# One GNN layer with a routed expert layer: the rows of x loaded in their own layout, rows scaled on ScalarE, transposes two tiles ahead, later shared pieces, and the self-loop on VectorE in three of four quarters

## What is computed

```python
deg = max((adj != 0).sum(-1), 1)
x = x + relu((A_norm @ ln(x) + ln(x)) @ W + b)      # A_norm = (adj + I) / deg of the row
x = x + moe(ln(x)) + gelu(ln(x) @ sw1.T) @ sw2.T    # top 1 of 8 experts: silu(w1) * w3, then w2
```

## Time and profile before

| | us |
|---|---|
| median of 3 runs (lowest, highest) | 485.64 (483.78, 487.36) |
| the profiled execution: its own time | 486.0 |
| its span | 484.4 |
| quarter 0, from the first z matmul to the self-loop | 10.35 to 53.70 |
| quarter 1, adjacency tiles | 54.70 to 87.50 |
| quarter 2, adjacency tiles | 114.8 to 139.9 |
| quarter 3, adjacency tiles | 167.7 to 192.9 |
| PE, DVE, ACT, POOL busy | 445.1, 270.8, 203.3, 336.5 |

### The profile page before, as it was taken

The page is one execution under the profiler, slowest core; times in us unless marked ns, Lnnn a source line. Parts: engine busy times, 40 slices in busy tenths (PEclk is TensorE's granted clock), DMA queues, the critical chain, the costliest instruction groups (busy, mean ns, idle before and its releaser), DMA issues.

```text
span 484.4 us, 8954 instructions
## 1 busy us (share of the span) xinstructions
PE 445.1 (92%) x2620; PEld 380.8 (79%) x2621; DVE 270.8 (56%) x549; ACT 203.3 (42%) x449; POOL 336.5 (69%) x309
## 2 busy tenths in 40 slices
PE   5899967999989999979988999999999999999992
PEld 5788845898869878868966888888888888888872
DVE  4998687654974498767773334233433333343330
ACT  3656458464545554574542233222323322232330
POOL 2888947276985799757796467976788579884112
PEclk9999999999999999999998999999999999999998
DMA  7565442201360055568676599997999563644000
GB/s 243 192 210 172 130 129 89 100 1 47 128 216 2 1 167 182 160 217 319 179 225 187 194 393 343 326 339 248 317 326 335 166 244 87 81 61 64 0 1 0
DMA packets 41004, 82.61 MB, mean 171 GB/s; under 512 B 5008, under 2 KB 16656, under 8 KB 38928
## 3 DMA queue, kind: packets, MB, share of 16 engines
q1 hardware_dynamic: 28416, 47.60, 30.1%
q0 software_dynamic: 7536, 29.39, 19.4%
q10 hardware_dynamic: 5024, 5.27, 3.7%
HBM read 74.74 MB, written 8.41 MB: 172 GB/s over the span
## 4 chain that ended last, share of the span: by engine, by line
PE 45%; POOL 19%; issue 9%; DMA 5%; DVE 3%; ACT 3%; SPq 2%; POOLq 1%; ACTq 0%
PE bank L1356 19%; POOL a_lo L447 10%; PE bank L1383 7%; POOL ering L493 5%; PE bank L1275 4%; PE bank L1297 4%; PE bank L1384 4%; DMA ering<-in_experts 3%; PE bank L1369 3%; POOL sorted_x L522 2%; PE bank L1299 2%; DMA eraw<-in_experts 2%; POOL gel_lo L463 2%; SPq L378 1%; ACT a_hi L605 1%
## 5 line engine op out<-in xcount | busy, mean ns | idle before, releaser
L1356 PE MATMUL bank<-ering,xsT_hi 128*128 x368 | 121.6, 402 | 1.9 <-POOL ering L493 1.8
L447 POOL TENSOR_TENSOR a_lo<-araw,a_hi 128x512 fp32r<-128x512 f32 x64 | 97.0, 1533 | 27.7 <-ACT a_hi L605 27.6
L1181 PE MATMUL bank<-zz,a_hi 128*128 128x512 f32 (+1 forms) x256 | 93.0, 402 | 9.8 <-POOL a_lo L447 9.6
L1100 DVE SCALAR_TENSOR_TENSOR hid<-bank,xs,sil 128x512 f32<-128x512 f32 x46 | 34.5, 751 | 92.5 <-ACT sil L740 90.5
L1356 PEld LDWEIGHTS bank<-ering,xsT_hi 128*128 128x128 f32 x368 | 69.9, 190 | 17.5 <-issue 2.7
L493 POOL TENSOR_TENSOR ering<-eraw,ering 128x512 fp32r<-128x512 f32 x40 | 51.9, 1317 | 29.7 <-DMA ering<-in_experts 20.1
L1356 PE MATMUL bank<-ering,xsT_lo 128*128 x184 | 72.4, 393 | 0.0
L1183 PE MATMUL bank<-zz,a_lo 128*128 128x256 f32 (+1 forms) x256 | 71.7, 280 | 0.0
L740 ACT ACTIVATE sil<-bank 128x512 f32<-128x512 f32 x46 | 27.5, 598 | 101.4 <-PE bank L1356 99.3
L1383 PE MATMUL bank<-ering,hidT_hi 128*128 x184 | 67.4, 406 | 1.2 <-DVE hidT_lo L1108 1.2
L1181 PEld LDWEIGHTS bank<-zz,a_hi 128*128 128x128 f32 x256 | 48.0, 188 | 24.2 <-issue 11.7
(11 more groups left out here) (156 smaller groups left out, 826.7 us busy)
## 6 DMA issues: line engine op xcount, KB each, us to landing
araw<-in_adj_t SPq DMA_DIRECT2D x32, 512.0 KB, 3.9
eraw<-in_experts SPq DMA_DIRECT2D x48, 256.0 KB, 5.0
ering<-in_experts POOLq DMA_DIRECT2D x8, 1536.0 KB, 9.0
eraw_more<-in_experts SPq DMA_DIRECT2D x48, 256.0 KB, 5.9
ering<-in_experts POOLq DMA_DIRECT2D x8, 1024.0 KB, 6.7
ering<-in_experts POOLq DMA_DIRECT2D x8, 512.0 KB, 4.8
xs<-sorted_x ACTq DMA_DIRECT2D x20, 129.0 KB, 4.7
resid<-in_x SPq DMA_DIRECT2D x4, 512.0 KB, 9.2
```

What stands on the lines that cost most here:

```text
L447: pool.tensor_tensor(a_lo[:, u % AR, :], araw[:, u // CJ, u % CJ, :], a_hi[:, u % AR, :].bitcast(F32), ALU.subtract).then_inc(adj_lo_ok, 1)
L1181: pe.matmul(acc(q, it)[:, :], a_hi[:, s, it * P:(it + 1) * P], zt, start=first, stop=False)
L1356: ins = pe.matmul(bank[2 * w + h][:, :], a[:, k, :], ering[:, bass.ds(slot, 1), part, at:at + BANK].rearrange("p a n -> p (a n)"), start=n ...
```

## The change

- **x's layout.** The host hands x as (128, 16, 256), so that a partition's rows of several tiles lie together; SP loads tile 0 alone, then tiles 1 to 3, and puts adjacency chunk 0 ahead of the second group.
- **Start.** Tile 0 is normalized alone, the split of W comes ahead of the identity's copy on ACT, and PE makes 10 instead of 20 transposes before it.
- **Rows on ScalarE.** For groups 1 to 3 DVE makes only the scale and the shift (`scales`), and ACT makes the rows as scale * x + shift (`scaled_rows`), three tiles ahead.
- **Transposes two ahead.** PE transposes tile t + 2 after `z_tile(t)`.
- **Bias and self-loop.** POOL no longer adds the bias. In quarters 0 to 2 PE does no `agg_end`, and DVE makes z * (1 + 1/deg) + bias in `first_products`; in quarter 3 the self-loop stays on PE and DVE adds the bias ahead of it (`add_bias`).
- **Shared pieces.** They begin two adjacency tiles later, with four banks for the first four pieces, so that pieces 0 to 3 wait for no earlier piece.
- **Places in the shared part.** Gate and rank steps of two stretches stand one block later, and the shared part waits for `rank_read` in one place only.

```diff
@@ -322,7 +325,7 @@
-            at = bank[2 + i % 2][:, :]
+            at = bank[(2, 3, 0, 1, 2, 3, 2, 3)[i]][:, :]
@@ -338,10 +341,8 @@
         def _(sp):
-            def rows_of_x(g):
-                sp.dma_start(resid[:, g * QT:(g + 1) * QT, :],
-                             x_in[g * QT * P:(g + 1) * QT * P, :].rearrange("(t p) d -> p t d", p=P)
-                             ).then_inc(x_loaded[g], 16)
+            def rows_of_x(first, last, loaded):
+                sp.dma_start(resid[:, first:last, :], x_in[:, first:last, :]).then_inc(loaded, 16)
@@ -353,11 +354,12 @@
-            rows_of_x(0)
+            rows_of_x(0, 1, x_first)
+            rows_of_x(1, QT, x_loaded[0])
...
+                chunk(0, c, c if c >= RAW else None)
...
-                    rows_of_x(c + 1)
-                chunk(0, c, c if c >= RAW else None)
+                    rows_of_x((c + 1) * QT, (c + 2) * QT, x_loaded[c + 1])
@@ -449,11 +451,8 @@
-                pool.wait_ge(bias_loaded, 16)
...
-                    pool.wait_ge(z_copied, t + 1)
-                    pool.tensor_tensor(norm[:, t, :], norm[:, t, :], bias[:], ALU.add).then_inc(bias_added, 1)
@@ -581,10 +580,17 @@
-            def stds(k):
-                act.wait_ge(var_ready, QT * (k + 1))
-                act.activation(std[:], mv[:, :, 1], ACT.Sqrt, bias=eps[:, 0:1]).then_inc(std_ready, 1)
+            def stds(k, first=0, last=QT):
+                act.wait_ge(var_ready, QT * k + last)
+                act.activation(std[:, first:last], mv[:, first:last, 1], ACT.Sqrt, bias=eps[:, 0:1]
+                               ).then_inc(std_ready, 1)
+            def scaled_rows(t):
+                act.wait_ge(scale_ready, t // QT)
+                act.activation(norm[:, t, :], resid[:, t, :], ACT.Identity, bias=shift[:, t % QT:t % QT + 1],
+                               scale=rstd[:, t % QT:t % QT + 1]).then_inc(ln_ready, 1)
@@ -606,21 +612,25 @@
             load_table(ACT.Sqrt)
-            stds(0)
-            act.wait_ge(consts, 1)
-            act.activation(ident_r[:], ident[:], ACT.Copy).then_inc(split_hi, 1)
+            stds(0, 0, 1)
             act.wait_ge(w_loaded, 16)
...
             xn_high(0)
+            stds(0, 1, QT)
+            act.wait_ge(consts, 1)
+            act.activation(ident_r[:], ident[:], ACT.Copy).then_inc(split_hi, 1)
+            xn_high(1)
...
             for t in range(NT):
-                if t % QT == 2 and t // QT + 1 < NQ:
+                if QT <= t + 3 < NT:
+                    scaled_rows(t + 3)
+                z_high(t)
+                if t + 2 < NT:
+                    xn_high(t + 2)
+                adj_high(t % (RAW * CJ), t // (RAW * CJ) + 1, t - AR + 1 if t >= AR else None)
+                if t % QT == 0 and t // QT + 1 < NQ:
                     stds(t // QT + 1)
-                if t + 1 < NT:
-                    xn_high(t + 1)
-                adj_high(t % (RAW * CJ), t // (RAW * CJ) + 1, t - AR + 1 if t >= AR else None)
-                z_high(t)
@@ -635,7 +645,10 @@
-                act.wait_ge(agg_sum, q + 1)
+                if q < NQ - 1:
+                    act.wait_ge(agg_tile, (q + 1) * NT)
+                else:
+                    act.wait_ge(agg_sum, 1)
@@ -682,8 +695,8 @@
-                if i >= 2:
-                    act.wait_ge(sw_lo_ok, i - 1)
+                if i >= 4:
+                    act.wait_ge(sw_lo_ok, i - (3 if i < 6 else 1))
@@ -693,13 +706,12 @@
                     split_gate()
-                for j in range(AR, TURN):
+                for j in range(AR, NT - 1):
                     adj_highs(q, j, j + 1)
-                    if q == 1:
-                        shared_piece_high(j - AR)
+                    if q == 1 and AR + 2 <= j < AR + 10:
+                        shared_piece_high(j - AR - 2)
                     if j == AR + 3:
                         stds(NQ + q - 1)
-                adj_highs(q, TURN, TURN + AR - 1)
                 xfT_highs(q - 1)
@@ -804,13 +816,21 @@
-                if first == 0:
-                    dve.wait_ge(std_ready, k + 1)
-                    chained(dve.reciprocal(rstd[:], std[:]))
-                    settle()
+                dve.wait_ge(std_ready, k + 2 if k > 0 else 1 if first == 0 else 2)
+                chained(dve.reciprocal(rstd[:, first:last], std[:, first:last]))
+                settle()
...
+            def scales(g):
+                dve.wait_ge(std_ready, g + 2)
+                dve.wait_ge(ln_ready, g * QT)
+                chained(dve.reciprocal(rstd[:], std[:]))
+                settle()
+                dve.scalar_tensor_tensor(shift[:], mv[:, :, 0], -1.0, rstd[:], ALU.mult, ALU.mult
+                                         ).then_inc(scale_ready, 1)
@@ -825,6 +845,13 @@
+            def add_bias(q):
+                dve.wait_ge(bias_loaded, 16)
+                dve.wait_ge(z_copied, (q + 1) * QT)
+                for t in group(q):
+                    chained(dve.tensor_tensor(norm[:, t, :], norm[:, t, :], bias[:], ALU.add))
@@ -836,27 +863,34 @@
-            dve.wait_ge(x_loaded[0], 16)
-            variances(group(0))
-            normalize(0, group(0))
+            dve.wait_ge(x_first, 16)
+            statistics(group(0), 0, 1)
+            aggregates(0, 1)
+            normalize(0, group(0), 0, 1)
...
-            dve.wait_ge(split_hi, 2)
+            dve.wait_ge(split_hi, 1)
...
+            dve.wait_ge(x_loaded[0], 16)
+            statistics(group(0), 1, QT)
+            aggregates(1, QT)
+            normalize(0, group(0), 1, QT)
+            xn_low(1)
...
-                if t + 1 < NT:
-                    xn_low(t + 1)
...
-                if g < NQ and i == 0:
-                    dve.wait_ge(x_loaded[g], 16)
-                    dve.wait_ge(ln_ready, g * QT)
-                if g < NQ and i < 2:
-                    statistics(group(g), 2 * i, 2 * i + 2)
-                elif g < NQ:
-                    normalize(g, group(g), 2 * (i - 2), 2 * (i - 1))
...
-                if g < NQ and i == 1:
+                if t + 2 < NT:
+                    xn_low(t + 2)
+                if i == 0 and g < NQ:
+                    if g == 1:
+                        dve.wait_ge(x_loaded[g], 16)
+                        dve.wait_ge(ln_ready, QT)
+                    statistics(group(g), 0 if g == 1 else 2, QT)
...
+                    scales(g)
+                elif i == QT - 1 and g + 1 < NQ:
+                    dve.wait_ge(x_loaded[g + 1], 16)
+                    statistics(group(g + 1), 0, 2)
@@ -888,7 +922,15 @@
-                dve.wait_ge(bias_added, (q + 1) * QT)
+                if q < NQ - 1:
+                    dve.wait_ge(bias_loaded, 16)
+                    dve.wait_ge(z_copied, (q + 1) * QT)
+                    chained(dve.tensor_scalar(self_part[:], dinv2[:], 1.0, None, ALU.add))
+                    settle()
+                    for it, t in enumerate(group(q)):
+                        chained(dve.scalar_tensor_tensor(norm[:, t, :], norm[:, t, :], self_part[:, it:it + 1],
+                                                         bias[:], ALU.mult, ALU.add))
+                settle()
@@ -1002,6 +1044,8 @@
+                if q == NQ - 1:
+                    add_bias(q)
@@ -1201,22 +1245,22 @@
-            keep_clock_up(20)
+            keep_clock_up(10)
...
-                if t + 1 < NT:
-                    xn_transpose(t + 1)
...
+                if t == 0:
+                    xn_transpose(1)
+                if t + 2 < NT:
+                    xn_transpose(t + 2)
...
-                agg_part(0, t, t % AR, t)
+                agg_part(0, t, t % AR, t, last=t == NT - 1)
...
-            pe.wait_ge(z_copied, NT)
-            agg_end(0)
@@ -1226,12 +1270,15 @@
-                    agg_part(q, j, j % AR, q * NT + j)
-                agg_end(q)
+                    agg_part(q, j, j % AR, q * NT + j, last=j == NT - 1 and q < NQ - 1)
+                if q == NQ - 1:
+                    agg_end(q)
...
-                if 0 < q < NQ - 1:
+                if q == 0:
+                    pe.wait_ge(sw_lo_ok, 4)
+                elif q < NQ - 1:
@@ -1283,7 +1330,8 @@
                     pe.wait_ge(agg_free, QT * min(hq // 2 + 2, NQ))
-                    pe.wait_ge(rank_read, min(hq // 2 + 1, NQ - 1))
+                    if hq == 2 * NQ - 3:
+                        pe.wait_ge(rank_read, NQ - 1)
                     if hq == 2 * NQ - 1:
@@ -1333,7 +1381,7 @@
-                    shared((q - 1) * 2 * NI, 2 * NI, {6: lambda: gate_back(q - 1), EARLY_RANKS_AT: lambda: ranks(q - 1)})
+                    shared((q - 1) * 2 * NI, 2 * NI, {7: lambda: gate_back(q - 1), EARLY_RANKS_AT: lambda: ranks(q - 1)})
@@ -1429,7 +1477,7 @@
-        "x": np.asarray(x),
+        "x": np.asarray(x).reshape(-1, P, x.shape[1]).transpose(1, 0, 2),
```

19 lines of the change are left out of this document (11 added, 8 removed).

## The result

The changed kernel takes 490.68 us (median; 489.75 to 491.89) against 486.04 in the same comparison: ratio 1.0101, 95% interval 1.0073 to 1.013. It is slower by 1%, where 479.5 was forecast, and the time lies outside the range. The profiled execution is the slowest of its four (491.89, span 490.2).

A forecast was written before the change was run, and what follows sets the result against it. It took a chain of waits headed by the experts' matmuls as the bound, with only the stretch up to 200 us open to change. 486.0 - 3.4 - 3.0 + 0.3 = 479.9, median 479.5 us; range 476.3 to 484.0.

The forecast's parts named there:

- Term 1, Start: Start of the front: first z near 7.2 us, tile 4's transpose at about 14.9 instead of 17.76.
- the rival by which the start gives nothing: Tile 0 lands no sooner than four tiles did; front gains only 0.8, time 482.1 us; chance 0.10.
- Term 1, Pace: Quarter 0: DVE's group falls from 10.65 to 7.9 us, under PE's 9.66; ScalarE has room for the rows.
- If those waits persist, ScalarE's wait for the scale would stand ahead of z's copies: Sign for the front: explains any PE waits over 0.5 us remaining at the transposes of tiles 8 and 12.
- Term 1, "GpSimd loses the bias ...: nothing": Front: taking the bias from GpSimd gains nothing, since nobody waited for it before the quarter's end.
- Term 2: Quarter 0's end to the shared part, through quarter 1: 32.9 us instead of 35.9, 3.0 less.
- the locks bite fully: Quarter 1: multiply-adds take 5.1 us beside GpSimd, gain shrinks to 0.5, time 482.0 us; chance 0.15.
- DVE fills up in quarter 1: VectorE's additions exceed its idle time; quarter 1 loses 6.7 us, quarter 3 loses 2, median 490.9; chance 0.05.
- Term 3: Quarters 2 and 3: quarter 2 gains nothing, VectorE's bias additions in quarter 3 cost 0.3 us.

The follow-up runs named there:

- e6: Changed kernel with a_hi first in each front tile on ScalarE and the next group's statistics one tile earlier: 487.2 us, ratio 1.0038.
- e3: Changed kernel with ScalarE making a_hi first instead of last in each tile of the front: 488.3 us, ratio 1.0056.
- e2: Kernel before plus only the VectorE self-loop in quarters 0 to 2 and VectorE's bias everywhere, GpSimd's bias additions gone: 491.8 us, ratio 1.0123.
- e5: e1 with a_hi first in each front tile and the next group's statistics one tile earlier: 483.6 us, ratio 0.9942.
- e8: e6 and e7 together, with quarter 3's bias through PSUM as well: 483.0 us, ratio 0.9931.
- e1: Changed kernel with the self-loop back on TensorE in all quarters and the bias back on GpSimd: 487.0 us, ratio 1.0023.
- e7: Changed kernel with the self-loop's products rewritten so that each of the eight has an operand in PSUM: 485.3 us, ratio 0.9992.
- e9: Kernel before plus only the later shared pieces, with own banks for the first four: 482.4 us, ratio 0.9939.
- e4: Changed kernel with the bias of tiles 12 to 15 added by GpSimd in the front instead of VectorE in quarter 3: 491.2 us, ratio 1.0099.
- e12: e11 with the twelve normalized rows of tiles 4 to 15 made by VectorE instead of ScalarE: 483.8 us, ratio 0.9967.
- e10: Changed kernel with 24 small matmuls adding zeros ahead of tile 7 of quarter 1, to keep PE at work: 490.9 us, ratio 1.0127.
- e11: Changed kernel with e6's front, VectorE self-loop only for quarter 1 in e7's form, bias shared between GpSimd and VectorE: 480.4 us, ratio 0.9891.

## Why the forecast was wrong

**Term 1, Start: right, 0.5 late.** T4 at 15.40 for 14.9, and the first z at 7.50 for 7.2; the rival by which the start gives nothing is out. The sum written down gives at most 14.0 + 0.63 = 14.6; the other 0.3 of the 14.9 had no source.

**Term 1, Pace: failed, 3.9 us.** From T4 to the end of quarter 0 are 39.14 us for 35.2. "ScalarE takes on 12 rows of at most 0.63, 7.6 us, on 25.7 busy of 43.35: room enough." The price of a row was right (0.60 to 0.65), ScalarE's busy time stayed under the sum (31.2 for 33.3), and there was room, as e6 shows with the same load. I had counted ScalarE by its sum and not by its queue. A root that waits for DVE's mv, then a row that waits for the scale, stood ahead of z's copies and of a_hi, so the wait of 1.0 that I charged to DVE's group was ScalarE's, and was passed to GpSimd and PE. e3 takes 2.8 of it back, e3's order with earlier statistics 4.15 (34.99 against 39.14). "If those waits persist, ScalarE's wait for the scale would stand ahead of z's copies" was half of it; I had not looked at where a_hi stands.

**Term 1, "GpSimd loses the bias ...: nothing": failed, and it hid part of the miss.** In the front of the kernel before, taking these additions out gave 1.1 (e2, 34.64 for 35.71). In the changed front they cost 1.8 to 1.9 (e5 against e8, e1 against e7), the last four of them 0.7, since the quarter ends in GpSimd's queue. The changed kernel's 39.14 has this gain in it. So it is partly luck that e6's 34.99 comes so near the 35.2 that I worked out: a gain of 1 to 2 us that I had put at nothing is in it, and what takes as much back is not shown.

**Term 2: failed, 5.3 us, by the size of one term and by one that I left out.** New rows were forecast 8.9 after the degrees, with 0.2 for the factor and 2.5 for the multiply-adds; they came after 13.3, with 1.25 and 5.76. The rest of the working came out. From the new rows to tile 13 are 18.2 us in the changed kernel, in e7 and in e8 (13.25 to 31.41, 9.16 to 27.33, 10.22 to 28.40), whatever PE's clock does between. e7, whose new rows come 9.2 after the degrees, took 32.84, where the forecast said 32.9. Behind tile 13 are 5.51 us, or 6.77 where the clock falls behind the wait of 2.27, as in the changed kernel: the other 1.3, which the term did not have. I took 2.5 by the normalizing row of this quarter, beside which GpSimd worked only part of the time, but the multiply-adds stand where GpSimd makes eight a_lo without a break. The bound at 5.1 was the row to take, since GpSimd was always at work beside it, and even that was low. With the pieces at their old place 2.5 would have been near (2.66 in e2).

The rival *the locks bite fully* had the mechanism and nearly the price (5.1). Its quarter 1 would be 35.4; the 2.8 to the measured 38.18 are the multiply-adds' other 0.7, the factor's 1.05 and the clock's 1.3, less 0.2. It let each later microsecond of the new rows count, and e1 and e9 bear that out: the pieces only just meet the new rows at their old time (0.51 and 0.52 of waiting). Its 482.0 still missed, mostly because it kept the front's gain. The Trainium skill (SBUF — State Buffer, Who interferes with whom) says that only the ports which VectorE and GpSimd share make them exclude each other. e7 agrees (0.42 a product with an operand in PSUM, where a multiply-add from SBUF took 1.44), and e2 shows that such a wait can strike a count or an instruction of four elements a row as well.

*DVE fills up in quarter 1* gave the right time (490.9) by luck: it had quarter 1 lose 6.7 and the front gain 3.4, where quarter 1 lost 2.3 and the front 1.1.

**Term 3: off by 0.5.** Quarter 2 gains 0.8 and gives it back, PE's first wait for gel_lo in quarter 3's stretch going from 0.76 to 1.78; that was forecast. The bias additions were 5.8, and cost 0.6 (e4) and not 0.3; the counts behind them, which then ran alone, gave part of it back (2.57 a pair, against 4.55 and 3.43 in e4).

The terms of the miss: start 0.5, pace 3.9, term 2 5.3, term 3 0.5, and 1.6 of the rest, which I take for this execution's spread: 11.8 of the 11.9 between 490.2 and the 478.3 that the forecast gives for the span.

**Not settled.** e1 to e12 don't say what makes the clock fall at one wait of 2.27 and not at another, nor why PE is slow up to 19.7 us in some executions.

## What to carry to other kernels

Before work is put on an engine with room, write down its queue for one tile and ask of each instruction that waits what stands behind it and who needs that; the busy share can't say. Put where GpSimd works without a break, a VectorE instruction that reads two SBUF tensors cost here about one GpSimd instruction (1.44 to 1.5), and even a factor of four elements a row took 1.25: give it an operand in PSUM where it can have one, or put it elsewhere. A price read from a row holds only for the GpSimd work that stood beside that row. When a gain and a loss are in one change, take them apart: the pieces alone, and the rows with another order, were each worth taking.

## What the runs showed of the hardware

- **The same wait, two clocks.** PE waits 2.26 to 2.28 us ahead of tile 13 in the changed kernel and in all the experiments but e2. From there to the degrees are 5.51 us in e3 and e7, 6.73 to 6.79 in the changed kernel, e4, e6, e8, e10, e11 and e12, and with `agg_end(1)` 6.41 and 6.43 in e1 and e5 but 7.76 in e9, whose granted clock of 80 to 85 us was 0.66. The Trainium skill (TensorE: Matmul & The Clock Gate, What's actually happening) has idle time bring the clock down. Here it does so in some executions only, and then costs 1.3; each kernel has one profiled execution, so whether it goes by the kernel is not shown.
- **A clock that its record does not show.** In e7 the a_hi matmuls take 0.63 and those of 256 columns 0.41 up to 19.7 us. The changed kernel shows the same lengths at 71.8 us, in a window whose granted clock is 0.50 (the level of 1.2 GHz); at the front it has 0.40 and 0.28 from 15.9 on, and 0.41 for z's until 14.3. The granted clock of 15 to 20 us is 1.00 in both. e8 has the same long durations there, and its record does show 0.54. e7's window:

```profile
15.00:20.00 5.00, 4.58 (x18) 4.20 (x19) 2.11 (x5) 4.03 (x12) 3.02 (x2) 1.00 0.17 63
```

  Read the durations there, not the column. The other starred executions (e1, e3, e4, e5, e11) read 1.00 too.
- **A lower clock that costs nothing.** In the changed kernel PE ran at 0.50 from 70 to 75 us, tiles 7 and 8 took 2.7 and 2.6 us instead of 1.41, and e10 shows that this had no price.
- **Which VectorE instructions wait beside GpSimd.** In quarter 3 of the changed kernel GpSimd makes its a_lo without a break from 173.81 to 192.56. VectorE's groups in that window (busy, mean ns of one):

```profile
L854 DVE TENSOR_TENSOR rows<-rows,bias 128x256 f32<-128x256 f32 x4 | 5.8, 1512 | 0.0
L807 DVE BATCH_NORM_STATS2 stats<-resid 128x6 f32<-128x256 f32 x4 | 1.4, 406 | 0.0
L820 DVE RECIPROCAL rstd<-std 128x4 f32<-128x4 f32 x1 | 0.2, 164 | 0.0
```

  The additions of two SBUF tensors take 5.8; the four statistics of the same width take what they took with GpSimd idle (1.41), and the reciprocal is as short as ever. So not every instruction on SBUF waits.
